# Opening of a four-layer graph kernel: two tiles made by a not-zero test, loads in another order, a run of products on zeros, bias products later

## What is computed

```python
x = _layernorm(x + _L0_gnn_ref(x, adj, L0_gnn_embedding, L0_gnn_weight, L0_gnn_bias), axis=-1)
x = _layernorm(x + _L1_gnn_ref(x, 0, L1_gnn_net_params, adj), axis=-1)
x = _layernorm(x + _L2_gnn_ref(x, adj, L2_gnn_weight_self, L2_gnn_weight_neighbor, L2_gnn_bias), axis=-1)
x = _layernorm(x + _L3_gnn_ref(x, adj, adj, L3_gnn_weight, L3_gnn_bias), axis=-1)
```

## Time and profile before

| | |
|---|---|
| median of 3 runs | 1243.95 us (1242.98 to 1246.37) |
| span of the profiled execution | 1241.0 us |
| TensorE busy | 1224.7 us (99%) |
| VectorE, ScalarE, GpSimd busy | 770.7, 212.8, 66.7 us (62%, 17%, 5%) |
| moved by DMA | 81.34 MB, mean 66 GB/s |

### The profile page before, as it was taken

How to read it: one execution, slowest core, us unless ns; L and a number is a source line. 1 busy time by engine, 2 the same in 40 slices (tenths; PEclk the granted TensorE clock), 3 DMA queues, 4 the chain that set the end, 5 groups by cost and what they waited for, 6 DMA issues and landing times.

```text
span 1241.0 us, 16426 instructions
## 1 busy us (share of the span) xinstructions
PE 1224.7 (99%) x5880; PEld 1027.3 (83%) x5880; DVE 770.7 (62%) x1875; ACT 212.8 (17%) x388; POOL 66.7 (5%) x54
## 2 busy tenths in 40 slices
PE   7999999999999999999999999999999999999997
PEld 6888888888888887888888888888888888888877
DVE  5825898887768877788635564472246355644725
ACT  5722111120111101220111111020111111110101
POOL 0000000000000000000000010010000000100100
PEclk9999999999999999999999999999999999999999
DMA  9832112231213110101011123033001111230331
GB/s 343 336 102 61 31 47 77 61 103 36 61 56 102 52 39 22 48 22 43 15 35 35 34 69 68 17 106 82 1 26 43 35 35 34 69 68 17 85 70 37
DMA packets 142329, 81.34 MB, mean 66 GB/s; under 512 B 110096, under 2 KB 121104, under 8 KB 140432
## 3 DMA queue, kind: packets, MB, share of 16 engines
q1 hardware_dynamic: 142240, 80.19, 22.5%
HBM read 55.00 MB, written 25.17 MB: 65 GB/s over the span
## 4 chain that ended last, share of the span: by engine, by line
PE 94%; DVE 3%; DMA 1%; SPq 1%; issue 1%; ACT 0%; DVEq 0%
PE ps L727 30%; PE ps L728 30%; PE ps L831 22%; PE ps L745 8%; PE ps L766 2%; PE ps L767 2%; DMA raw<-in_at 1%; DVE ring L1103 1%; DVE nat L1103 1%; PE ps L739 1%; SPq L1149 0%; DVE sml L1043 0%; DMA ring_x<-y1d 0%; DVE sml L1034 0%; DVE nat L1038 0%
## 5 line engine op out<-in xcount | busy, mean ns | idle before, releaser
L727 PE MATMUL ps<-B,xs 128*128 128x512 f32 (+1 forms) x1680 | 656.3, 391 | 1.5 <-DVE xs L993 1.5
L728 PE MATMUL ps<-B,xs 128*128 128x512 f32 (+1 forms) x1680 | 649.4, 387 | 0.0
L727 PEld LDWEIGHTS ps<-B,xs 128*128 128x128 f32 x1680 | 315.8, 188 | 63.6 <-issue 1.6
L728 PEld LDWEIGHTS ps<-B,xs 128*128 128x128 f32 x1680 | 315.7, 188 | 61.8
L831 PE MATMUL ps<-Tw,xs 128*128 128x512 f32 x1280 | 309.0, 391 | 1.0 <-DVE ring L1103 1.0
L831 PEld LDWEIGHTS ps<-Tw,xs 128*128 128x128 f32 x1280 | 238.8, 188 | 54.3 <-DVE ring L1103 5.0
L981 DVE TENSOR_TENSOR ring<-ps,rrep 128x512 f32<-128x512 f32 (+1 forms) x95 | 64.6, 684 | 241.8 <-PE ps L728 230.7
L1103 DVE SCALAR_TENSOR_TENSOR nat<-ps,embn,nat 128x128 f32<-128x128 f32 x448 | 153.9, 344 | 43.2 <-PE ps L831 43.0
L1103 DVE SCALAR_TENSOR_TENSOR ring<-ps,embn,ring 128x128 f32<-128x128 f32 x512 | 175.7, 343 | 0.0
L745 PEld LDWEIGHTS ps<-W,ring 128*128 128x128 f32 x896 | 111.6, 191 | 7.5 <-DVE ring L981 1.9
L745 PE MATMUL ps<-W,ring 128*128 128x128 f32 x896 | 113.3, 275 | 0.7 <-DVE ring L981 0.6
(11 more groups left out here) (68 smaller groups left out, 546.4 us busy)
## 6 DMA issues: line engine op xcount, KB each, us to landing
raw<-in_at SPq DMA_DIRECT2D x13, 1024.0 KB, 16.3
td<-ring SPq DMA_DIRECT2D x32, 256.0 KB, 2.0
ring<-td SPq DMA_DIRECT2D x128, 64.0 KB, 2.6
ring<-in_xn SPq DMA_DIRECT2D x16, 256.0 KB, 2.8
ring_x<-in_xt SPq DMA_DIRECT2D x32, 128.0 KB, 3.1
ring_x<-y1d SPq DMA_DIRECT2D x32, 128.0 KB, 3.2
out<-nat SPq DMA_DIRECT2D x15, 256.0 KB, 2.4
y1d<-ring SPq DMA_DIRECT2D x14, 256.0 KB, 2.8
```

The costliest lines, as they stand in the source:

```text
L727: pe.matmul(bank, x[:, 0, m, :], of, start=m == 0, stop=False)
L728: mm = pe.matmul(bank, x[:, 1, m, :], of, start=False, stop=ends and m == NT - 1)
```

## The change

Five things are done, all of them in the opening.

1. Tiles 0 and 1 become patterns by "raw is not 0" on VectorE (L984 of the new file), without `rrep` and without a wait for ScalarE. Their comparison with `rrep`, which now only counts, is a step of its own, "equal" (L996), after tile 7 and after tile 10.
2. Tiles 0 to 7 are loaded to other slots of `raw` (`SLOT`: 14, 15, 8 to 13), so that their patterns are not written in place, and VectorE no longer waits for ScalarE's count. Tiles 8 to 15 are in place as before, and their loads wait until the tile that had their slot is done with (`BEFORE`): tiles 14 and 15 for the two "equal" steps.
3. Loads: x chunk 0 of pair 0 and piece 0 of tile 0 come first, then x of pair 1, the embedding and the bias matrix, the rest of tile 0, tile 1; `rrep` comes in two halves with tile 2. Tiles 2, 3 and 4 are loaded and made in halves. Counting is in the pieces of `COUNTED`; tile 0 and tile 1 are counted whole.
4. TensorE first waits for VectorE to zero a part of `ring_g`, then runs 10 matmuls on it (`WARM`) into bank 7. Nobody reads their result.
5. The bias matmuls follow the products of tile 0, block 0.

The diff, without the lists of semaphores:

```diff
--- before.py
+++ after.py
@@ -24,9 +24,17 @@
 SPAN = [(512 * c, 512) for c in range(NC)] + [(1536, 256), (1792, 256)]
-PIECES = {0: 4, 1: 2, LAST: 4}
-COUNT = [sum(PIECES.get(i, 1) for i in range(m)) for m in range(17)]
+PIECES = {0: 4, 1: 2, 2: 2, 3: 2, 4: 2, LAST: 4}
+COUNTED = {2: 2, 3: 2, 4: 2, LAST: 4}
+COUNT = [sum(COUNTED.get(i, 1) for i in range(m)) for m in range(17)]
+SLOT = [14, 15, 8, 9, 10, 11, 12, 13] + list(range(8, NT))
+BEFORE = {SLOT[m]: m for m in range(8)}
+WARM = 10
@@ -224,16 +232,24 @@
         for m in range(NT):
-            if m % 4 == 0:
+            if m % 4 == 0 and m:
                 put("split", 0, 0, m // 4)
                 put("split", 1, 0, m // 4)
-            for c in range(PIECES.get(m, 1)):
+            elif m == 0:
+                put("tile", 0, 0, 0, 0)
+                put("split", 0, 0, 0)
+                put("split", 1, 0, 0)
+            for c in range(COUNTED.get(m, 1)):
+                put("sign", 0, 0, c, m)
+            for c in range(0 if m else 1, PIECES.get(m, 1)):
                 put("tile", 0, 0, c, m)
-            if m == 0:
-                put("bias")
+            if m == 7 or m == 10:
+                put("equal", 0, 0, 0, 0 if m == 7 else 1)
             of = [(j, c) for c in range(NC) for j in range(2) if j == 0 or c < 2 or m < 12]
             for j, c in sorted(of) if m == LAST else of:
                 put("first", j, 0, c, m)
+                if (j, c, m) == (1, 0, 0):
+                    put("bias")
             if m == LAST:
                 for c in range(NC):
                     put("scale", 0, 0, c)
@@ -624,11 +640,18 @@
             def tile_landed(m, c):
-                return (s_at[m][c], 16) if s_at[m] else (s_at[m - 7][c], 32)
+                if m == LAST:
+                    return s_at[0][c], 32
+                return (s_at[m][c], 16) if m < 8 else (s_at[m - 7][0], 32)
             def piece(k, c):
                 width = N // PIECES.get(k, 1)
+                return slice(c * width, (c + 1) * width)
+            def counted(k, c):
+                width = N // COUNTED.get(k, 1)
                 return slice(c * width, (c + 1) * width)
             def span(c):
@@ -751,6 +774,11 @@
                     j, p, c, k, n = s.j, s.p, s.c, s.k, s.j % 2
                     y = y_slot(j, p, c)
                     if s == STEPS[0] and not general:
+                        pe.wait_ge(s_zero, 1)
+                        for _ in range(WARM):
+                            pe.matmul(ps[:, 7, :], ring_g[:, 0:64].bitcast(BF16), ring_g[:, 0:256].bitcast(BF16),
+                                      start=True, stop=True)
+                    if s.kind == "bias" and not general:
                         pe.wait_ge(s_e, 32)
                         for t in range(NT):
                             mm = pe.matmul(ps[:, 3 + t // 8 * 4, (t % 8) * C:(t % 8 + 1) * C], embt_s[:, t * P:(t + 1) * P],
@@ -847,12 +875,13 @@
                         ac.wait_ge(s_b0, 1)
                         for i in range(2):
                             ac.copy(bcopy[:, i * 512:(i + 1) * 512], ps[:, 3 + 4 * i, :]).then_inc(s_b0c, 1)
-                    if s.kind == "tile" and not general:
-                        cols = piece(k, c)
-                        ac.wait_ge(*tile_landed(k, c))
-                        if tile_at[s] > 2:
-                            ac.wait_ge(s_nz, tile_at[s] - 2)
-                        ac.activation(junk[:, tile_at[s] % 2, cols], raw[:, k, cols].bitcast(U32), ACT.Sign,
+                    if s.kind == "sign" and not general:
+                        cols, v = counted(k, c), sign_at[s]
+                        for i in range(c, c + 1) if k in COUNTED else range(PIECES.get(k, 1)):
+                            ac.wait_ge(*tile_landed(k, i))
+                        if v > 2:
+                            ac.wait_ge(s_nz, v - 2)
+                        ac.activation(junk[:, v % 2, cols], raw[:, SLOT[k], cols].bitcast(U32), ACT.Sign,
                                       accum_out=cnt[:, 1, COUNT[k] + c:COUNT[k] + c + 1]).then_inc(s_nz, 1)
                     if s.kind == "split":
                         src, there, v = source_of(j, p, c)
@@ -946,15 +975,30 @@
                     j, p, c, k, n = s.j, s.p, s.c, s.k, s.j % 2
                     v, g, sm = ch(nat[n], c), groups(nat[n], c), sml[:, n, c % NC, :, 0:SPAN[c][1] // C]
                     wide = [P, SPAN[c][1] // C, C]
+                    if s == STEPS[0] and not general:
+                        dv.memset(ring_g[:, 0:256], 0.0).then_inc(s_zero, 1)
                     if s.kind == "tile" and not general:
-                        cols = piece(k, c)
-                        for i in range(NC) if k else [c]:
+                        cols, there = piece(k, c), raw[:, SLOT[k], piece(k, c)]
+                        dv.wait_ge(*tile_landed(k, c))
+                        if k < 2:
+                            dv.tensor_scalar(B[:, k, cols], there, 0.0, None, ALU.not_equal, ALU.bypass).then_inc(s_B, 1)
+                            continue
+                        for i in range(2) if PIECES.get(k, 1) != 2 else [c]:
                             dv.wait_ge(s_r[i], 16)
-                        dv.wait_ge(s_nz, tile_at[s])
-                        dv.scalar_tensor_tensor(B[:, k, cols], raw[:, k, cols], 1.0, rrep[:, cols], ALU.mult, ALU.is_equal,
+                        if SLOT[k] == k:
+                            dv.wait_ge(s_nz, sign_at[s._replace(kind="sign")])
+                        dv.scalar_tensor_tensor(B[:, k, cols], there, 1.0, rrep[:, cols], ALU.mult, ALU.is_equal,
                                                 accum_out=cnt[:, 0, COUNT[k] + c:COUNT[k] + c + 1]).then_inc(s_B, 1)
+                    if s.kind == "equal" and not general:
+                        there = raw[:, SLOT[k], :]
+                        dv.wait_ge(s_nz, sign_at[Step("sign", 0, 0, 0, k)])
+                        dv.wait_ge(s_B, tile_at[Step("tile", 0, 0, PIECES.get(k, 1) - 1, k)])
+                        dv.scalar_tensor_tensor(there, there, 1.0, rrep[:], ALU.mult, ALU.is_equal,
+                                                accum_out=cnt[:, 0, COUNT[k]:COUNT[k] + 1]).then_inc(s_eq, 1)
                     if s.kind == "flag" and not general:
                         dv.wait_ge(s_B, len(tile_at))
+                        dv.wait_ge(s_eq, 2)
+                        dv.wait_ge(s_nz, len(sign_at))
                         dv.wait_ge(s_const, 48)
                         dv.tensor_tensor(odd[:, 0:COUNT[NT]], cnt[:, 0, :], cnt[:, 1, :], ALU.not_equal).then_inc(s_chk, 1)
                         dv.tensor_scalar(odd[:, COUNT[NT]:], r16s[:], 0.0, None, ALU.is_equal, ALU.bypass).then_inc(s_chk, 1)
@@ -1136,19 +1180,26 @@
             def sp_load(sp):
+                sp.dma_start(ch(nat[0], 0), xn[0, :, span(0)]).then_inc(s_x[0], 16)
+                sp.dma_start(raw[:, SLOT[0], piece(0, 0)], at[0:P, piece(0, 0)]).then_inc(s_at[0][0], 16)
+                sp.dma_start(ch(nat[1], 0), xn[1, :, span(0)]).then_inc(s_x[0], 16)
                 sp.dma_start(embt_s, embt).then_inc(s_e, 16)
                 sp.dma_start(b0t[:], b0).then_inc(s_e, 16)
                 for m in range(NT):
-                    if m % 4 == 0:
+                    if m % 4 == 0 and m:
                         for j in range(2):
                             sp.dma_start(ch(nat[j], m // 4), xn[j, :, m * P:(m + 4) * P]).then_inc(s_x[m // 4], 16)
-                    if not s_at[m]:
-                        sp.wait_ge(s_nz, tile_at[Step("tile", 0, 0, 0, m - 7)])
-                    for c in range(PIECES.get(m, 1)):
+                    if m >= 8:
+                        gone = max(BEFORE[m], m - 7) if m < LAST else BEFORE[m]
+                        sp.wait_ge(s_nz, sign_at[Step("sign", 0, 0, COUNTED.get(gone, 1) - 1, gone)])
+                        sp.wait_ge(s_B, tile_at[Step("tile", 0, 0, PIECES.get(gone, 1) - 1, gone)])
+                        if BEFORE[m] < 2:
+                            sp.wait_ge(s_eq, BEFORE[m] + 1)
+                    for c in range(0 if m else 1, PIECES.get(m, 1)):
                         cols = piece(m, c)
-                        sp.dma_start(raw[:, m, cols], at[m * P:(m + 1) * P, cols]).then_inc(tile_landed(m, c)[0], 16)
-                        if m == 0:
+                        if m == 2:
                             sp.dma_start(rrep[:, cols], rb[:, cols]).then_inc(s_r[c], 16)
+                        sp.dma_start(raw[:, SLOT[m], cols], at[m * P:(m + 1) * P, cols]).then_inc(tile_landed(m, c)[0], 16)
                     if m == 6:
                         sp.dma_start(identf[:], eye).then_inc(s_const, 16)
                         sp.dma_start(epst[:], eps).then_inc(s_const, 16)
```

(10 more changed lines are left out.)

## The result

The changed kernel takes 1246.63 us (median of 16 runs, 1244.61 to 1247.39) against 1244.53 for the one before (16 runs): a ratio of 1.0014, with a 95% interval of 1.0007 to 1.0020. It is slower by some 2 us, where 4.3 us less were forecast (1239.6 us, between 1238.0 and 1243.8).

What follows compares the result with a forecast made beforehand. TensorE bounds the kernel (busy 1224.7 of 1241.0 us), with time to win before tile 2. Gain 4.8 us there, capped to 4.4 by VectorE, less 0.1 for small things: 1243.95 becomes 1239.6 us, range 1238.0 to 1243.8.

Steps and rivals of the forecast that it cites:

- Bias: I take 3.5: Bias matmuls behind the first products: 3.5 us at the higher clock, half the 7.0 seen, from 8.0 to 11.5 us.
- I take it that they raise it: Opening on TensorE: ten matmuls on zeros, 4.3 us long, raise the clock; 4.0 us of products had done so.
- rival A: Opening: clock does not hold; low throughout, tile 2 at 23.8, 1244.4 us; falling mid-bias, 1242; chance 0.25 for both.
- First product at 6.9: TensorE's first real product: x lands at 5.7, then ScalarE's cast 0.6 and VectorE's rest 0.65 us.
- Block 3 behind ScalarE's copies at 13.9: Tile 0's block 3: piece 3 lands at 10.7, count takes 2.1, two copies 1.05, so ready at 13.9 us.
- rival E: Opening loads: piece 3 lands by 9.5 and tile 7 by 31; gain 5.5, 1238.4 us, chance 0.05.
- this chain, and not the bias, sets the rest: Tile 0, block 3: ScalarE's count and copies end at 13.9, later than TensorE's 13.3 us, and set tile 2's start.
- The sum from 18.5 to 25.3 us for tile 2: Start of tile 2, forecast at 18.5 us instead of 23.31, a gain of 4.8 us there.
- VectorE's tile 8 at 41.2: VectorE's pattern for tile 8, forecast ready at 40.2 to 41.4 us.
- The start of tile 2: TensorE runs through from there, so kernel time moves by as much as this start, unless a later tile comes late.
- The cap at tile 8: VectorE's row of work before tile 8 caps the gain at 3.9 to 5.1 us, middle 4.4, replacing 4.8.
- The median of the runs stands 2.95 us above the span: Conversion for the whole kernel: 2.95 us added to the profile's span, so 1236.7 becomes 1239.6 us.

Runs made afterwards that it cites:

- bias late: Changed kernel with the bias behind 24 matmuls of tiles 0 and 1, whose block 3 follows blocks 0 and 1 of tile 2: 1245.27 us, ratio 1.0004.
- 24 zeros: Changed kernel with 24 matmuls on zeros in place of 10: 1243.01 us, ratio 0.9995 to the kernel before.
- x together: Changed kernel with the x chunks of both pairs loaded together, piece 0 of tile 0 behind them: 1245.11 us, ratio 1.0009.
- bias first: Changed kernel without zeros, bias matmuls back ahead of all products and their inputs loaded first: 1241.53 us, ratio 0.9979.
- no zeros: Changed kernel without the ten matmuls on zeros, nothing else: 1247.12 us, ratio 1.0024.
- no bias: Changed kernel without the 16 bias matmuls, so the bias is missing from its result: 1240.38 us, ratio 0.9963.
- bias split: Changed kernel without zeros, 13 bias matmuls ahead of all products, 3 behind block 2 of tile 1, block 3 of tiles 0 and 1 later: 1241.41 us.
- before, bias moved: The kernel before with only the bias matmuls moved behind the products of tile 0, block 0: 1248.19 us, ratio 1.0025.
- mixed: Changed kernel, bias inputs loaded first; after ten zeros, bias in groups of 4, one zeros matmul behind each, ahead of all products: 1242.26 us.
- no bias, counts later: Changed kernel without the bias matmuls and with the "equal" steps after tiles 8 and 11: 1240.82 us, ratio 0.9967.

## Why the prediction was wrong, step by step

- *"Bias: I take 3.5"*, and before it *"I take it that they raise it"*. This is the step that failed, in both halves. The ten zeros did not bring a high clock to the first product, 2.9 us after the last of them, and the bias took 7.0 us instead of 3.5. The size at the higher level was right (3.7, bias late), but the clock falls during the bias or at its end. The 7 us of bias in front of products at the lower level had been the hint. I read it as "does not raise the clock" and did not ask whether it holds it; that was open, and the runs with 24 zeros and with the bias late show that it does not. The outcome was the first form of rival A, low all through, which had a part of a chance of 0.25.
- *"First product at 6.9."* It came at 8.5: x landed at 6.95, not 5.7. I had counted only when it was issued, and not what was put between. That is 1.25 us of the 1.6. The other 0.3 are the two handovers, at which I had put nothing: VectorE began 0.73 us after ScalarE's cast (0.6 in the sum), TensorE 0.83 after VectorE (0.65).
- *Block 3 behind ScalarE's copies at 13.9.* The count of tile 0 started at 9.48, since piece 3 landed near 9.5, the early end of my bounds and the condition of rival E; in the changed kernel the copies waited 6.1 us for the bias instead. So "this chain, and not the bias, sets the rest" was wrong as well: the bias did.
- *The sum from 18.5 to 25.3 us for tile 2:* first product +1.6; the first four matmuls at the lower level +0.9; bias +3.5; then 28 matmuls in 7.8 us, where block 3's wait and the rest had been given 7.0, +0.8. That is 6.8 us.
- *Rival A's price,* "tile 2 at 23.8, no gain at all", was too low by 1.5 us, mainly since it had the first product at 6.9. The range ended at 1243.8, even below that price of 1244.4.
- *Right:* the stalls in front of tile 2 vanish, VectorE's tile 8 at 41.2, the second half of tile 2 at 18.5 (a little ahead of the 18.8 to 20.1), the loads behind the new waits cost nothing, and the waits behind 24 us stay at 3.9. The start of tile 2 did set the rest: it is 2.0 us later, the mark 1.85 and the median 2.1.
- *The cap at tile 8* was a true bound (without the bias and with a high clock it was met with 0.1 us to spare), but it cost nothing in any run. The sum of 4.4 us rested on this term. Its price for one pass of VectorE, 2.4 us from tile to tile, was too high: the changed kernel shows 2.21 (38.90 to 41.11), the "equal" steps too.
- *"The median of the runs stands 2.95 us above the span"* compared the median with an execution that was 1 us faster. In each execution of the later runs the time is 1.8 to 2.0 us above its own span. It cancels in the forecast, which adds the same 2.95 back.

## What to carry to other kernels

Work that is free beside the first loads is not free once it stands behind the first real product: ask what a moved block hid behind, and price it at the slowest rate at which it has been seen. A busy TensorE is not one that keeps its clock: small matmuls (here 16 rows, 64 columns) neither raised nor held it in one stretch, while the same ones in groups of 1 us with 1.1 us of full products between them did no harm, and with 0.2 us between them they did. And when the order of the first loads is changed, the one that the first product needs last decides, so nothing goes in between.

## What was not expected of the hardware

- The clock's rise is scattered. From the start of an unbroken run of full products to the first at the higher spacing it took 4.4 us (before), 3.0 (changed), 4.4 (bias first), 4.8 (24 zeros), 6.0 (no zeros; no bias), 5.1 and 3.5 (bias late, ahead of the bias and behind it), 3.5 (bias split), 3.4 (before, bias moved), 5.9 (mixed), 5.6 (no bias, counts later) and 3.1 (x together). With 7 to 14 matmuls at 0.2 us extra each, that alone moves one profiled execution of this kernel by over 1 us (estimated from these rows: 7 x 0.2 = 1.4), so marks within 1 us of each other do not rank two kernels.
- A gap can undo the zeros. In the run without the bias the ten zeros took 3.90 us instead of 4.45, so the clock had risen by their end; the granted clock went to 0.50 near 7.8 us, in a gap of 3.62 us, and the products behind it were 0.43 apart. In the run with x together the gap was 1.95 us, and the four products before the bias still came at the higher level (durations of 0.40 to 0.49 us, where the lower level shows 0.63); but the clock went to 0.50 at 8.4 us, during the last of them, and the bias behind them took 7.0 us again. The Trainium skill (TensorE: Matmul & The Clock Gate, "HAM oscillation") has this rule, that waiting between bursts brings the lower level back. The run without the bias agrees with it; the run with x together agrees only in part, since its clock fell 1.1 us after TensorE had taken up work again. It was the rule I had weighed and given 0.25. That section names waiting as the cause; the fall during unbroken bias matmuls is beyond what it says there.
- An x chunk landed 2.0 us later for 256 KB issued between it and the first one. The other runs bear it out: with the bias inputs loaded first, the cast starts at 5.87 and 5.83 us where nothing stands between the chunks (before; before, bias moved), and at 7.27 to 8.26 where the piece does (bias first, split, mixed). Why so much is open: it was not tried with other sizes.
